# A Mamba, S5 and expert-layer kernel: a sum on VectorE and most sums on GpSimd two slots later, S5 matrices made earlier

## What is computed

```python
x = x + mamba(layernorm(x), ...)    # 256 channels, 64 states each
x = x + experts(layernorm(x), ...)
x = x + s5(layernorm(x), ...)
x = x + experts(layernorm(x), ...)

# mamba: for each of 256 x 64 (channel, state), over 512 steps
delta = softplus(d_raw @ Wdt + bdt);  A = -exp(A_log)
h = exp(delta_t * A) * h + (delta_t * B_t) * x_t
y = (C_t * sum(h) + xs * Dp) * silu(res)
z = y @ Wo + bo + residual;  out = gamma * norm(z) + beta

# experts: combine[n, e] is 0 but for the two best experts of row n
y = (silu(x @ W1[e]) * (x @ W2[e])) @ W3[e];  out = sum_e combine[:, e] * y
```

## Time and profile before

| | |
|---|---|
| median of 3 runs | 1831.92 us (1828.08 to 1833.31) |
| profiled execution | 1833.74 us, its span 1831.9 us |
| DVE busy | 1535.7 us, 84% |
| POOL busy | 1497.5 us, 82% |
| PE busy | 1348.5 us, 74% |
| ACT busy | 1264.5 us, 69% |
| scans (DVE, line 1275) | 1024, 1191.1 us |
| products (POOL, line 956) | 512, 1192.4 us |
| decays (ACT, line 853) | 1024, 680.8 us |
| expert sums (POOL, line 899) | 120, 152.5 us |

### The profile page before, as it was taken

The page is one execution under the profiler, slowest core; times in us unless marked ns, Lnnn a source line. Parts: engine busy times, 40 slices in busy tenths (PEclk is TensorE's granted clock), DMA queues, the critical chain, the costliest instruction groups (busy, mean ns, idle before and its releaser), DMA issues. The chain is left out here.

```text
span 1831.9 us, 19041 instructions
## 1 busy us (share of the span) xinstructions
PE 1348.5 (74%) x5928; PEld 612.4 (33%) x5928; DVE 1535.7 (84%) x2154; ACT 1264.5 (69%) x2227; POOL 1497.5 (82%) x876
## 2 busy tenths in 40 slices
PE   5336468678866888778876887768876878668958
PEld 1001123234332433224332343324332343225525
DVE  3999988988899888998999888998999888995232
ACT  4558568777877678786886868777777777664413
POOL 0999989879998799978998899977998899984212
PEclk9556679888998989889897989989898989889969
DMA  3511411131113211122111310132101401100000
GB/s 117 192 52 50 165 46 52 50 123 67 58 47 104 89 52 52 49 92 98 58 46 56 137 52 29 55 109 98 50 32 50 164 29 49 46 29 1 6 1 6
DMA packets 38747, 121.89 MB, mean 67 GB/s; under 512 B 5875, under 2 KB 21110, under 8 KB 26358
## 3 DMA queue, kind: packets, MB, share of 16 engines
q1 hardware_dynamic: 37062, 120.67, 18.5%
q10 hardware_dynamic: 1584, 0.01, 0.0%
HBM read 109.13 MB, written 11.53 MB: 66 GB/s over the span
## 5 line engine op out<-in xcount | busy, mean ns | idle before, releaser
L1275 DVE TENSOR_TENSOR_SCAN h<-da,w 128x512 f32<-128x512 f32 x1024 | 1191.1, 1210 | 111.2 <-ACT da L853 94.5
L956 POOL TENSOR_TENSOR w<-ur,br 128x1024 f32<-128x1024 f32 x512 | 1192.4, 2360 | 29.9 <-DVE h L1275 17.5
L853 ACT ACTIVATE da<-dr,al 128x511 f32<-128x511 f32 x1024 | 680.8, 686 | 245.0 <-DVE h L1275 242.9
L646 PE MATMUL ys<-h,wsum 128*32 128x512 f32 x2048 | 315.4, 692 | 186.7 <-DVE h L1275 167.4
L580 PE MATMUL bankH<-nT,w 128*128 128x512 f32 x512 | 304.5, 679 | 98.5 <-DVE aq L1199 92.8
L899 POOL TENSOR_TENSOR x<-x,yk 128x512 f32<-128x512 f32 x120 | 152.5, 1271 | 181.4 <-ACT yk L815 181.4
L592 PEld LDWEIGHTS bankY<-w,aq 128*128 128x128 f32 x2048 | 250.6, 195 | 85.4 <-issue 75.8
L592 PE MATMUL bankY<-w,aq 128*128 128x128 f32 x2048 | 258.1, 280 | 12.4 <-DVE aq L1199 7.9
L580 PE MATMUL bankG<-nT,w 128*128 128x512 f32 x432 | 249.8, 662 | 16.4 <-DVE aq L1199 16.4
L815 ACT ACTIVATE yk<-bankY,rt 128x128 f32<-128x128 f32 x480 | 140.8, 360 | 86.6 <-PE bankY L592 77.5
L580 PEld LDWEIGHTS bankH<-nT,w 128*128 128x128 f32 x512 | 86.4, 203 | 258.0 <-DVE aq L1199 165.1
(11 more groups left out here) (188 smaller groups left out, 1156.0 us busy)
## 6 DMA issues: line engine op xcount, KB each, us to landing
br<-b_rows SPq DMA_DIRECT2D x64, 1024.0 KB, 5.0
dr<-d_rows SPq DMA_DIRECT2D x16, 1024.0 KB, 7.4
ur<-u_rows SPq DMA_DIRECT2D x16, 1024.0 KB, 8.4
d_rows<-vh SPq DMA_DIRECT2D x16, 256.0 KB
u_rows<-th SPq DMA_DIRECT2D x16, 256.0 KB
xnew<-in_L_attn_a_x_dram SPq DMA_DIRECT2D x8, 256.0 KB, 5.3
w<-in_L_ffn_W_dram SPq DMA_DIRECT2D x2, 1024.0 KB, 11.1
x<-in_L_attn_a_x_dram SPq DMA_DIRECT2D x8, 256.0 KB, 9.0
```

Of the source, the lines that this page charges most:

```text
L646: ins = nc.tensor.matmul(ys[32 * q:32 * q + 32, :], wsum[:, :], h[:, (DUOS * b + 2 * group + q // 2) % H_RING, q % 2, :], start=(n == 0), ...
L853: A(da[duo % D_RING][:, k % 2, 1:L], dr[:, half, q, 1:L], ACT.Exp, scale=nega[:, QUADS * half + q, n:n + 1]).then_inc(decay_ready, 1)
L956: G.tensor_tensor(w[:, turn_duo % W_RING, :, :], ur[:, half, q:q + 2, :], br[:, chunk % B_RING, row:row + 1, :].to_broadcast([128, 2, L]), ...
L1275: V.tensor_tensor_scan(h[:, turn_duo % H_RING, k % 2, :], da[duo % D_RING][:, k % 2, :], w[:, turn_duo % W_RING, k % 2, :], 0.0, ALU.mult, ...
```

## The change

Three things are moved, and nothing is added or taken away. DVE adds `z` at slot 9 instead of 7. POOL's sums of the experts are due 8 slots after the product with `w3` instead of 6, except that of expert 6 of the first layer. The S5 matrices are made at slot 81 of the start instead of 87, their transposes come at 80 instead of 87, and the copy to `bcs`, which stood ahead, is now due at 87.

```diff
-WEIGH_LAG, SUM_LAG = 3, 6
+WEIGH_LAG, SUM_LAG, LONG_LAG = 3, 6, 8
...
-SETUP_ROWS_AT = PRE_AT + 9
-SETUP_AT = PRE_AT + 17
-MATRICES_AT = PRE_AT + 17
+SETUP_ROWS_AT, ROWS_AT = PRE_AT + 9, PRE_AT + 17
+SETUP_AT = PRE_AT + 11
+MATRICES_AT = PRE_AT + 10
...
                     if on_vector(m, e):
                         continue
-                    yield SLOT[f"y{m}_{e}"] + SUM_LAG
+                    yield SLOT[f"y{m}_{e}"] + (SUM_LAG if (m, e) == (1, E - 2) else LONG_LAG)
                     pool.wait_ge(weighted, 3 * (sums_before(c, m) + e + 1))
...
                 chain(V.tensor_scalar(nega[:, :, :], al[:, :, :], -1.0, None, ALU.mult))
+                yield ROWS_AT
                 v.wait_ge(rows_spread, 1)
...
                 yield from take_sums(c, 1, t, TAKE_AT)
-                yield SLOT["z"] + 2
+                yield SLOT["z"] + 4
                 p = got(t, "z")
```

## The result

| | before | after |
|---|---|---|
| median of 4 runs each | 1832.62 us (1828.08 to 1842.61) | 1862.35 us (1861.77 to 1862.63) |
| profiled execution, its span | 1833.74, 1831.9 us | 1861.77, 1860.0 us |
| turn 0 | 156.50 us | 162.31 us |
| turn 1 | 201.70 | 202.80 |
| turns 2 to 6 | 208.50, 211.31, 208.50, 211.33, 208.53 | 214.60, 214.95, 215.09, 215.00, 215.07 |

The changed kernel is slower: 1.0154 times the time of before, with a 95% interval of 1.0112 to 1.0196. 1854 was predicted, with a range of 1838 to 1865. A turn's length is the time from its first scan to the next turn's. The kernel before has executions at two levels in every group of runs, 1828 to 1836 and 1838 to 1843 us (9 of 29 at the upper one in the largest group); its profile is of the lower one.

A forecast was written before the change was run, and what follows sets the result against it. It saw no engine full, but four engines handing work round in a ring with little lead. Terms 0 + 1.3 + 3 x 2.7 + 3 x 4.0 + 1.0 = 22.4 us gave 1854 us on the median 1831.92, range 1838 to 1865.

The forecast's parts named there:

- the main forecast: Whole kernel: 22.4 us slower, 1854 us, its own range 1846 to 1860, chance 0.50.
- start: S5 matrices made earlier: first scan 5.2 us sooner, given back by scan 56, so 0 us.
- turn 1: No late experts there; `z` moves by two scans (2.2 us) and POOL ends 1.3 us later.
- turns 2, 4 and 6: Scan 32 comes 4.0 us later, 1.3 is absorbed before scans 56 and 71: +2.7 us a turn.
- turns 3, 5 and 7: Scan 32 comes 4.0 us later and nothing is absorbed, ACT and TensorE being as late as DVE: +4.0 a turn.
- tail: After the last turn `z` comes 1.4 us later and bank Y 0.6 later; taken as +1.0 us.
- z: DVE's add of `z`, behind `aq` of tile g2_10, comes 2.6 us later; POOL passes on 1.7 us.
- The sums: At y2_5 and y2_6 ACT's weighing waits for POOL's sum, a product later: +2.3 us, with `z` +4.0.
- DVE's gap at scan 32: DVE's idle time before the scan behind the first expert layer's chain: to grow from 2.92 to 5 or 6 us.
- From scan 32 to the end of the turn: Turns 2, 4 and 6 absorb 1.3 of 4.0 us at scans 56 and 71; turns 3, 5 and 7 none.
- the second rival, slow clock: Turns 2, 4 and 6 also fall to the lower clock before scan 32, 3 x 2.83 = 8.5 us more: 1863, chance 0.20.
- The rule on gaps: Basis of the first rival: two scans fill DVE's 3.25 us gap before `z`, 17.6 us faster, 1814 us, chance 0.11.

The follow-up runs named there:

- sums alone: The kernel before with only POOL's expert sums two slots later (expert 6 of the first layer excepted): 1843.59 us, ratio 1.0056.
- the second buffer: The changed kernel with two `yk` buffers in turn, and `bst` in two parts instead of five: 1840.60 us, ratio 1.0030.
- `z` alone: The kernel before with only DVE's add of `z` two slots later: median 1854.58 us, ratio 1.0109, four executions from 1842.97 to 1863.64.
- `z` ahead of g2_10: The changed kernel with `z` added at slot 8 instead of 9, ahead of DVE's product `aq` of tile g2_10: 1841.20 us, ratio 1.0029.

## Why the prediction was right, and where not

**The sign and the mechanism.** Both cost mechanisms are shown, each by one run that has it alone and one that takes it away: sums alone +11.9 us and the second buffer -21.8; `z` alone +11 to +32 and `z` ahead of g2_10 -21.2; both taken away give the time of the kernel before with that buffer. The time lies inside the range, but outside the 1846 to 1860 that I had given the main forecast itself.

**The sum, term by term.** It gave 22.4 us, and the two profiled executions differ by 28.0. Predicted and then measured: start 0 and -3.4; turn 1 +1.3 and +1.1; turns 2, 4 and 6 together +8.1 and +19.2; turns 3, 5 and 7 together +12.0 and +12.7; tail +1.0 and -1.6. That the total missed by only 5.6 us is partly luck: the start and the tail came out 6.0 us lower than given, and the even turns 11.1 higher.

**Start: right.** 0 was predicted, 0.9998 measured. In the profiled executions turn 1 starts 3.4 us sooner (207.48 against 210.86), because POOL's first product does (42.57 against 46.77). That isn't the change: the kernel before with the second `yk`, whose start is the old one, has it at 43.51, and the other profiles with the old start at 42.6 to 44.5. The execution of the earlier trace rows had a late start. The first part of the mechanism is in these rows of the changed kernel, DVE:

```profile
22.15 0.21 DVE L1075 TENSOR_SCALAR nrm<-nrm 64x128 f32<-64x128 f32 x1
...
28.09 0.55 DVE L1014 COPY bcs<-ys 128x384 f32<-128x384 f32 x1
...
110.06 4.64 DVE L1276 TENSOR_TENSOR_SCAN h<-da,w 128x512 f32<-128x512 f32 x4 [2.41 <-issue]
```

The matrices are made in the idle stretch, and what is won at scan 0 is given back where DVE has caught up with POOL: the gap of 1.84 us at 114.27 is 2.41, and three more of 1.19 stand beside it.

**z: right in its place, a little low at the end of its chain.** Predicted +2.6 and DVE's idle time 3.1; measured +2.65 and 3.08. POOL was to wait about 5 us for the moments: 4.93. What it passes on to the transposes was set at 1.7; `z` alone shows 2.1. The term that was too large is POOL's 0.93 us of idle time before `nrm`, which was to be swallowed whole. 0.42 us of it stays, since POOL waits there for DVE's factors, and these now take 4.39 us instead of 2.09, held up behind POOL's own instructions.

**The sums: right.** +2.3 at the transposes, measured 2.3 alone. Together 4.0 was predicted and 4.4 measured. DVE's gap at scan 32 was to grow to 5 or 6 us and is 3.7 to 4.0: that sign missed. DVE comes later to that gap than was thought, by the 2.3 us more that it spends on the factors and by 0.5 to 0.9 us of new idle time behind scan 29.

**From scan 32 to the end of the turn: this step failed.** In turns 3 and 5 the sum gave +4.0, and +3.6 and +3.7 came. In turns 2, 4 and 6 it gave +2.7, and +6.1, +6.6 and +6.5 came. Of the 3.7 us between, 0.4 are the transposes; about 1.8 are the chain to scan 32, 9.85 us before and 11.4 to 11.8 now; 1.3 are the part that was to be absorbed at scans 56 and 71, and 0.2 come behind. Nothing was absorbed, though those two gaps did close. Turn 4 of the changed kernel:

```profile
935.46 1.22 DVE L1276 TENSOR_TENSOR_SCAN h<-da,w 128x512 f32<-128x512 f32 x1 [1.95 <-ACT da L853]
...
945.80 1.74 PE L580 MATMUL bankH<-nT,w 128*128 128x512 f32 x2 [2.74 <-DVE aq L1200]
947.33 1.91 PE L580 MATMUL bankG<-nT,w 128*128 128x512 f32 x2
...
953.87 1.22 DVE L1276 TENSOR_TENSOR_SCAN h<-da,w 128x512 f32<-128x512 f32 x1 [2.47 <-ACT da L853]
```

These are scans 54 and 65, whose gaps were 1.12 and 0.77 us in turn 4 of before. The gaps at scans 52, 54 and 56 (0.72, 1.12 and 0.69) have become one of 1.95, and the 0.64 at scan 71 is gone: 1.2 us are absorbed, about as predicted. The gap at scan 65 takes 1.7 back. The tiles ahead of it run at the lower clock (1.91 us a pair, 1.02 at the higher). The 8 us from the first of these tiles on, in turn 4 of before and then of the changed kernel (busy us of PE, PEld, DVE, ACT and POOL, granted clock, DMA share, GB/s):

```profile
932.99:940.99 8.00, 8.00 (x36) 4.06 (x36) 7.20 (x14) 7.42 (x11) 8.00 (x5) 1.00 0.33 134
```

```profile
945.80:953.80 8.00, 8.00 (x25) 3.38 (x26) 5.56 (x12) 5.76 (x9) 8.00 (x5) 0.79 0.35 134
```

PE idled about as long ahead of them in both, 2.94 and 2.74 us. The kernel with four added matmuls separates slack and clock. In its turns 2, 5 and 6 the gap at scan 54 is 1.95 too, but that at scan 65 is 0.77, and from scan 32 to the end the turn takes 150.9 to 151.3 us, against 152.6 in turn 4 of before and 152.8 in that of the changed kernel. So the slack was there, and the lower clock used it up. With `z` alone it wasn't even touched: the gaps at scans 56 and 71 are 0.70 and 0.65, and the turns are 3.1 us longer than the short ones of before.

So the second rival, slow clock, was what happened in the even turns, and its time of 1863 is nearer than mine; but it had put the whole 2.83 us at scan 32, where 1.8 came, and it had left the 1.3 absorbed. That its sum fits to 1 us is partly chance. The error of the main forecast is that step: a gap that stood in the trace of one turn was taken for time won after the shift, while the lower clock opened another behind it. The turns of about 211 and 215 us that were to be seen were all of 214.6 to 215.1. The prediction had treated the clock as a matter of one stretch; in the odd turns of before it had already widened the gap at scan 54 (2.83 us in turn 5 after 10 us at a mean clock of 0.83, 1.12 in turn 4 after 10 us at 1.00).

**Turn 7 and the tail.** Predicted 4.0 and 1.0. Turn 7 took 5.3 more, and from its last scan on the kernel took 165.5 us, 1.6 less than before (167.1): the transposes of x1 come 2.0 later (35.8 against 33.8 after the last scan), and what follows makes up for it. No run takes the tail apart. But it takes 167.1 us in before and 162.3 in before with the second `yk`, both with the old place of `z`, and 167.2 with the buffer and `z` at slot 8, so the 1.6 us can't be put down to the change.

**The rule on gaps.** The Trainium skill, Perfetto Trace Analysis, "Optimization Strategy", has one look for gaps on the most-contended engine and let what blocks them start sooner. With `z` at slot 8 one half of it was tried: scan 8 in DVE's gap was free, but brought nothing that was measured. DVE is busy 84% of the time, and the wait that counted was one on ACT, busy 69%. There a second buffer, which lets what blocks start sooner, gave 12 us; the transposes came 0.86 us sooner a turn, and the rest came with the clock.

## What to carry to other kernels

Before an instruction is moved behind "idle time", look at what else stands in that idle time on the same engine: two slots later put `z` behind a product that itself waits, and one slot later it would have been free. A single buffer between two engines is a handshake both ways; the small row of it (9.1 us, each wait 1.0 us or less) shows that it is already tight, and then every delay of the consumer is passed on whole (2.3 us of 2.3 here). Idle time of one engine just ahead of another's result isn't slack where the other may be held up by it: POOL's 0.93 us before `nrm` were swallowed only by half. Where a matmul chain of some microseconds lies on the path, read the granted clock along the entire turn, ahead of it and behind, before giving a gap as slack.

## What the runs showed of the hardware that I had not expected

Each turn of these kernels has stretches at the lower of the two clock levels (1.2 GHz), and they don't fall at the same place in every turn and kernel. In before they alternate with a turn's parity; with the earlier start alone the parity is exchanged. In the changed kernel the lengths of the turns from the second on are within 0.5 us, but the place still alternates: besides the stretch ahead of scan 32 there is one ahead of scan 54 in turns 3 and 5 (DVE's gap there is 3.64 us, 1.95 in the others), and one ahead of scan 65 in turns 2, 4 and 6 (2.47 us, 0.77 in the others). Such a stretch costs 1.7 us either way. In four others (`z` alone, and the three with two `yk` and no added matmuls) these turns are alike in both. The Trainium skill, TensorE: Matmul & The Clock Gate, "What's actually happening", says that the monitor behind the clock runs free of the kernel and isn't reset when one starts, so that the place of a transition varies from run to run. The exchanged parity agrees with it, though each kernel has only one profile; no run here shows the monitor itself.

The size of it: the same 744 matmul records of a turn take PE 162 us in the short turns of before and 165.3 in the long ones; the chain from the transposes to the decay of scan 32 takes from 8.3 to 12.2 us in turns 2 to 7 of these kernels; and added, useless matmuls made the changed kernel 16 us faster and the one with two buffers 15 us slower.

And DVE's `TENSOR_SCALAR` of 128x128, which takes 0.34 us beside an idle POOL, took up to 2.4 us here, ending 0.1 us after the `TENSOR_TENSOR` that POOL was running. Over the kernel the 32 of them took 17.6 us before and 33.3 after the change, with nothing altered in them.
